# The FP4 weights' last product on GpSimd, and their maxima as the first steps of the NF4 loop's FP4 chain

## What is computed

```
x = x + LN(x) @ (weight * blockmask).T
x = x + LN(x) @ (int4 * scale).T + bias
x = x + L1_attn(LN(x))       # weights are NF4 codes * scales, plus LoRA, d_ff 1792
x = x + L1_ffn(LN(x))        # weights and activations rounded to FP4, d_ff 1376
```

```
s  = max(max|w| / 2688, 1e-12)                # one number for the whole matrix
sb = clip(max|w/s| over 16 columns / 6, ...)  # one number per block of 16
q  = nearest FP4 level of w/s/sb
dq = q * sb * s                               # the last product; the last 128 columns stay w
```

## Time and profile before

| | us |
|---|---|
| runs: lowest, median, highest of 3 | 808.89, 811.8, 812.21 |
| the profiled execution's own time | 808.92 |
| its span, first to last instruction | 807.6 |
| TensorE busy | 723.5 (90%) |
| VectorE busy | 576.0 (71%) |
| ScalarE busy | 444.6 (55%) |
| GpSimd busy | 188.6 (23%) |
| mean granted TensorE clock | 0.960 of full speed |

### The profile page before, as it was taken

The page is one execution under the profiler, slowest core; times in us unless marked ns, Lnnn a source line. Parts: engine busy times, 40 slices in busy tenths (PEclk is TensorE's granted clock), DMA queues, the critical chain, the costliest instruction groups (busy, mean ns, idle before and its releaser), DMA issues.

```text
span 807.6 us, 11305 instructions
## 1 busy us (share of the span) xinstructions
PE 723.5 (90%) x4136; PEld 538.1 (67%) x4136; DVE 576.0 (71%) x1087; ACT 444.6 (55%) x579; POOL 188.6 (23%) x174
## 2 busy tenths in 40 slices
PE   1899766988999998989998999988899999989998
PEld 1666522656777765666665777766677788967886
DVE  5979967563597788879799887666654434578883
ACT  3777877565777677876875632254433211335452
POOL 1013000004263543626356343211401000000000
PEclk9999956999999999999998999998999999989999
DMA  9637678766466676767665310302211010200001
GB/s 342 186 124 210 209 262 266 262 205 231 128 201 196 196 244 210 230 198 240 230 196 162 109 40 32 83 1 66 81 37 48 25 39 14 75 2 14 26 27 40
DMA packets 55543, 110.82 MB, mean 137 GB/s; under 512 B 9904, under 2 KB 20560, under 8 KB 55232
## 3 DMA queue, kind: packets, MB, share of 16 engines
q1 hardware_dynamic: 42912, 80.27, 31.0%
q10 hardware_dynamic: 8192, 15.73, 6.1%
q0 software_dynamic: 4384, 14.09, 5.9%
HBM read 92.17 MB, written 17.89 MB: 136 GB/s over the span
## 4 chain that ended last, share of the span: by engine, by line
PE 53%; DVE 24%; issue 9%; ACT 8%; DMA 4%; ACTq 1%; POOL 0%; SPq 0%; DVEq 0%; POOLq 0%
PE bank L1198 14%; PE bank L1199 13%; PE bank L1200 13%; PE bank L1306 3%; ACT hot L1615 2%; DVE hot L1876 2%; DMA wide_buf<-in_down_flat 2%; DVE x L1999 2%; DVE bank L1902 2%; DVE q_a L1949 1%; PE bank L1319 1%; PE bank L1504 1%; ACT c L1574 1%; DVE q_r L1943 1%; DVE stats L1798 1%
## 5 line engine op out<-in xcount | busy, mean ns | idle before, releaser
L1615 ACT ACTIVATE hot<-rep,levels 128x2048 f16<-128x2048 f16 x94 | 189.5, 2056 | 15.2 <-ACT c L1574 11.7
L1198 PE MATMUL bank<-zt_h,w_h 128*128 128x512 f32 (+1 forms) x232 | 93.2, 402 | 2.5 <-DVE zt_l L1987 2.0
L1200 PE MATMUL bank<-zt_h,w_l 128*128 128x512 f32 (+1 forms) x232 | 91.0, 392 | 0.0
L1199 PE MATMUL bank<-zt_l,w_h 128*128 128x512 f32 (+1 forms) x232 | 90.8, 392 | 0.0
L1306 PE MATMUL bank<-hot,diag 128*32 128x512 f16 x1160 | 78.7, 402 | 2.2 <-ACT hot L1615 2.2
L1198 PE MATMUL bank<-w_h,xq_h 128*128 128x512 f32 (+1 forms) x192 | 73.8, 385 | 2.3 <-ACT xq_l L1707 1.9
L1199 PE MATMUL bank<-w_l,xq_h 128*128 128x512 f32 (+1 forms) x192 | 71.9, 374 | 0.0
L1200 PE MATMUL bank<-w_h,xq_l 128*128 128x512 f32 (+1 forms) x192 | 71.7, 374 | 0.0
L2143 POOL TENSOR_TENSOR q_a<-q_a,q_m 128x384 f32<-128x384 f32 (+3 forms) x34 | 35.7, 1051 | 106.7 <-DVE q_m L1762 106.7
L1306 PEld LDWEIGHTS bank<-hot,diag 128*32 128x32 f16 x1160 | 26.4, 99 | 45.8 <-issue 24.9
L2199 POOL TENSOR_TENSOR at_l<-ztok,at_h 128x512 fp32r<-128x512 f32 x28 | 37.4, 1336 | 70.4 <-ACT at_h L1647 70.3
(11 more groups left out here) (221 smaller groups left out, 1692.0 us busy)
## 6 DMA issues: line engine op xcount, KB each, us to landing
rep<-codes SPq DMA_DIRECT2D x56, 512.0 KB, 4.7
codes<-c SPq DMA_DIRECT2D x28, 256.0 KB
raw<-in_codes_gu_t ACTq DMA_DIRECT2D x14, 512.0 KB, 5.4
sc<-in_scales_gu_t SPq DMA_DIRECT2D x56, 128.0 KB, 4.3
raw<-in_codes_attn_t ACTq DMA_DIRECT2D x7, 512.0 KB, 4.0
raw<-in_codes_down_t ACTq DMA_DIRECT2D x7, 512.0 KB, 5.3
sc<-in_scales_down_t SPq DMA_DIRECT2D x28, 128.0 KB, 3.1
wide_buf<-in_gate_flat SPq DMA_DIRECT2D x5, 512.0 KB, 4.4
```

What stands on the lines that cost most here:

```text
L1198: PE.matmul(psum, lh, rh, start=first, stop=False, **kw)
L1199: PE.matmul(psum, lh, rl, start=False, stop=False, **kw)
L1200: return PE.matmul(psum, ll, rh, start=False, stop=last, **kw)
L1615: S.activation(hots[plan.slot[hot_ring(t), (t, m)]][:], codes_in_place(t), ACT.Relu, bias=bias, scale=slope).then_inc(sem("ramp_act"), 1)
```

## The change

1. maxima() is no longer woven into stages() and attention(). It is chained ahead of fp4_weights(), as one side of the NF4 loop: its 20 yields and the 78 others are 98 for the loop's 100 main steps, and FP4_RATE goes from 0.8 to 1.0.
2. wround on GpSimd gets a third instruction, the last product. VectorE's wfinish is gone. For w_down, VectorE multiplies the block factors by mscale ahead of it (12 small instructions). The two temporary buffers (q_tmp) are freed by GpSimd's product, and SP's store waits for GpSimd.

```diff
-MAX_RATE = 1.0
-FP4_RATE = 0.8
+FP4_RATE = 1.0
...
-                p.take("q_tmp", 2, ("w", name, c, o), ("dve", "wfinish", name, c, o))
+                p.take("q_tmp", 2, ("w", name, c, o), ("pool", "wfinish", name, c, o))
...
-    fp4, greatest = fp4_weights(), maxima()
+    fp4 = itertools.chain(maxima(), fp4_weights())
...
-    side_max = Side(greatest, MAX_RATE)
-    weave(stages(), Side(itertools.chain(int4_weights(), greatest), INT4_RATE), Side(ready_nf4, EARLY_RATE))
-    until(n_attn - 1, side_max)
+    weave(stages(), Side(int4_weights(), INT4_RATE), Side(ready_nf4, EARLY_RATE))
+    until(n_attn - 1)
...
-    weave(attention(), Side(ready_nf4, ATT_RATE), side_max)
-    drain(greatest)
+    weave(attention(), Side(ready_nf4, ATT_RATE))
...
                 reciprocals(rb, cb)
+                if name == "down":
+                    V.tensor_scalar(cb, cb, mscale[:, o:o + 1], None, ALU.mult)
...
-            elif kind == "wfinish":
...
-                if name == "down":
-                    ins = V.scalar_tensor_tensor(blocks_of(wide, nq), blocks_of(ua, nq), mscale[:, o:o + 1], part,
-                                                 ALU.mult, ALU.mult)
-                else:
-                    ins = V.tensor_tensor(blocks_of(wide, nq), blocks_of(ua, nq), part, ALU.mult)
-                ins.then_inc(sem("wfinish_dve"), 1)
...
-                round_off(ua, um, nq, done("dve", "wround", *key), own).then_inc(sem("wround_pool"), 1)
+                own.up(round_off(ua, um, nq, done("dve", "wround", *key), own))
+                own.wait_ge()
+                for m in vacant("q_out", ("w", *key)):
+                    pool.wait_ge(*m)
+                G.tensor_tensor(blocks_of(q_out[plan.slot["q_out", ("w", *key)]][0:orow, :], nq), blocks_of(ua, nq),
+                                spread_of(cc[:, 0:nq // FP4_BLOCK], orow, nq), ALU.mult).then_inc(
+                                    sem("wfinish_pool"), 1)
...
-                sp.wait_ge(*done("dve", "wfinish", *key))
+                sp.wait_ge(*done("dve", "wread", *key))
+                sp.wait_ge(*done("pool", "wfinish", *key))
```

More of the change, by code:

```diff
@@ L1248, in row_buf, with blocks_of, spread_of @@
         return late_bufs[plan.slot["late", ("row", c, i)]]
+    def blocks_of(t, nq):
+        return t[:, 0:nq].rearrange("p (b c) -> p b c", c=FP4_BLOCK)
+    def spread_of(t, rows, nq):
+        return t.unsqueeze(2).broadcast_to([rows, nq // FP4_BLOCK, FP4_BLOCK])
     def wround_size(name, c, o):
@@ L1749, in reciprocals @@
             steady.wait_ge()
[L1751 to L1755, removed]
         def magic(ua, um, nq):
@@ L2193, in pool_program @@
                 orow, w, nq = wround_size(*key)
-                ua, um, _, _ = (v[0:orow, :] for v in q_tmp[plan.slot["q_tmp", ("w", *key)]])
-                round_off(ua, um, nq, done("dve", "wround", *key), own).then_inc(sem("wround_pool"), 1)
+                ua, um, cc, _ = (v[0:orow, :] for v in q_tmp[plan.slot["q_tmp", ("w", *key)]])
+                own.up(round_off(ua, um, nq, done("dve", "wround", *key), own))
[5 more added lines that the diff above has]
+                                    sem("wfinish_pool"), 1)
             elif kind == "gu_mul":
```

## The result

The changed kernel takes **817.75 us** in the median (six runs, 815.5 to 821.84) against 810.85 for the kernel before (six runs, 808.75 to 813.14) on the same chip: ratio 1.009, 95% interval [1.0064, 1.0115]. It is slower, where I had forecast no change at 811.7; the time lies in the range of 801 to 821. The profiled execution took 817.39 us with a span of 816.1, against 808.92 and 807.6.

A forecast was written before the change was run, and what follows sets the result against it. No engine was full from 60 to 139 us; TensorE was full in the loop's first 20 steps, then 225.7 of 241.7 us. Terms -1.2 - 4.5 + 9 - 1.4 + 2.5 - 4.5 = -0.1 gave 811.7 us, range 801 to 821.

The forecast's parts named there:

- The stages and attention: Before the loop, VectorE loses 18 reductions of the maxima: -1.2 us in the stages, -4.5 in attention as TensorE's gaps go.
- The loads in the head: Loop's first 20 steps: late landings of the maxima's parts cost TensorE +9 us; a gap going with the moved roundings, -1.4.
- The gather: First gather, now at step 21 behind the maximum over partitions, is wanted at step 22: TensorE waits, +2.5 us.
- The pause of GpSimd behind the gathers: GpSimd's at_l and rounding wait behind eight indirect DMAs (10 us) but are used several steps later: 0.
- The dense part: Loop's next 80 steps: product moves to GpSimd, VectorE's load hardly falls but its peaks do, so TensorE waits less: -4.5 us.
- My own sign for this: Sign of a wrong forecast: the loop's 80 steps after the first 20 take longer than 241.7 us.
- L1902's gaps: Sign of a right forecast: TensorE's waits for L1902 after the loop's first 20 steps are near 6.5 us.
- The rival with the comparisons: GpSimd blocks VectorE's comparisons, which lose 13 us instead of 2; 80 later steps cost +0.5, not -4.5: 816.7 us, chance 0.10.
- The head at the pace of the loads: Slower rival: landing, issue and reduction exceed 6.9 us, costing 13.5 in the loop's first 20 steps: 822.2 us, chance 0.22.
- the first rival: Faster rival: loads hidden, peaks were what counted; first 20 loop steps cost +1.5, the next 80 give 8: 799.7 us, chance 0.28.

The follow-up runs named there:

- four halves: The changed kernel with four halves of buffer instead of two for the maxima's parts, loads going out three parts ahead: 808.01 us, ratio 0.995.

## Why the prediction was wrong

**The stages and attention** (forecast -1.2 and -4.5): the stages' boundary moved by under 1 us and attention gave the rest of -6.1. Of the gaps of the earlier trace rows behind late parts 0.7 us is left. Right.

**The loads in the head** (+9 - 1.4): the difference is right, +7.7, by errors that cancel, which is luck. The idle time rose by 6.4 us (1.4 to 7.8), where I had 7.6; even this term had a miscount in it, for between 153 and 178 us the trace has six reductions and not seven, which makes 0.87 us a part and 10.5 for the head instead of 9. The same matmuls at a lower clock cost 4.8 us more, which no term of the sum had. And 32 transposes of seven or eight tiles left the head, worth some 3.5 us (67.88 - 64.39), which I neither credited here nor charged to the dense part.

**The gather** (+2.5): TensorE waited 1.4 us for it. Inside the bounds. The pause of GpSimd behind the gathers, which I had at 0, cost about 1 us of the dense part by the traces, too little for the times to tell.

**The dense part** (-4.5) is the step that failed: "So its load there hardly falls, since the higher rate gives back what the move takes. What falls is the peak". For VectorE's load I had 199.7 us, and 2 of contention, against 203.3; the measured load rose by 8.4 us, for seven tiles cost 29 us on VectorE with the stalls of all the others, where 2.96 each made 20.7. And equal load was not no cost: the waits for L1899 grew by 5.5 us where I had taken away 4.5. Measured one at a time, the product gives -3.5 us in the dense part, near my -4.5 though only 2.0 of it are waits for L1902. The seven tiles brought there, with the higher rate, give +12.3 (259.0 with four halves against 246.7): 6.7 of busy TensorE, of which 3 to 5 are their 29 transposes, and 5.6 of idle, of which 1.3 are the wait for the first gather. That is 1.8 us a tile, 1.4 without that wait and the pause, where in the head seven tiles cost 0.6 each (68.7 against 64.4). I had priced the seven tiles and the higher rate at nothing for TensorE. My own sign for this stood in the prediction: a dense part longer than before. L1902's gaps there were to be 6.5 us and were 16.5.

In one sum, going from kernel to kernel by their traces: the product -4.1 in the loop (319.5 to 315.4), the tiles moved out of the head, with the maxima in their place and the higher rate, +8.0 (315.4 to 323.4), the late loads +11.9 (323.4 to 335.3), the start -6.1 and the end -1.2: +8.5 us.

**The rivals.** The rival with the comparisons named nearly the right time, 816.7, and the right stage, but the wrong cause: with the product alone moved the dense part became 3.5 us shorter, and at the new rate 9.1 us. That its time fits is luck. The comparisons lost 3.4 us more than before, where it had them lose 13; more went to the small scalings of each tile (L1751 and L1943), 129 and 99 ns more in the mean for 34 tiles. The Trainium skill, "SBUF — State Buffer", Who interferes with whom, has it that when a VectorE instruction in a two-port mode and a GpSimd one meet, the later is blocked until the other is done. The trace agrees in that 11 of the 13 long L1751 ended 0.03 to 0.04 us after a GpSimd instruction; in which mode they ran no run here shows. With the product alone moved, 11 us of the 28.5 that it freed came back in other instructions or were its mscale products. The head at the pace of the loads (822.2) did not come, since VectorE waited at seven of the 18 parts only.

The kernel with the loads hidden, four halves, came to a ratio of 0.995, not the 0.985 of the first rival: its head was as hoped for, its dense part not.

## What to carry over

When side work is moved from one stretch of a loop to another, price the work pushed out of its old place as well: a rounding tile cost 0.6 us of TensorE's time in the steps where VectorE had room and 1.4 to 1.8 where it was at 84%. A double-buffered load that waits for its predecessor but one in an in-order queue needs its landing, and the queue's other waits, to fit into the distance; here two more halves, otherwise idle, were worth 11 us with the maxima in the loop (ratio 1.009 to 0.995) and 5.9 with them in attention. And of two edits that arrive together, time each alone: one was worth -0.9%, the other +1.6%.

## What the runs showed of the hardware

- **A gap can cost twice.** The granted clock read 0.66 in the 5 us behind a gap of 2.87 us of TensorE, and a head with 7.8 us of idle time needed 4.8 us more for the same matmuls than one with none (69.15 and 64.39 us). Behind the 2.30 us gap at 171 us in the kernel before it stayed at 1.00.
- **GpSimd paused for 8.95 us** between gathers that follow a partition all-reduce and its next plain addition; with a plain copy in the all-reduce's place the addition starts 0.97 us after the last gather's start. In the kernel before the addition came 8.07 us after the last gather, but there the trace has it waiting for ScalarE's at_h, so whether it paused can't be seen.
- **VectorE's small instructions stall behind GpSimd's running ones.** One of them, a scaling of 14 to 32 elements a partition (L1751), took 174 ns at the least and 1167 at the most; in 11 of the 13 long cases it ended 0.03 to 0.04 us after a GpSimd instruction that had begun before it.
- **A product with a broadcast operand was no dearer on GpSimd than an addition.** The groups of its three instructions in the changed kernel, for 384 elements:

```profile
L2131 POOL TENSOR_TENSOR q_a<-q_a,q_m 128x384 f32<-128x384 f32 x20 | 22.0, 1102 | 1.6
L2128 POOL TENSOR_TENSOR q_a<-q_a,q_m 128x384 f32<-128x384 f32 x20 | 20.4, 1019 | 31.8 <-DVE q_m L1759 31.7
L2184 POOL TENSOR_TENSOR q_d<-q_a,q_c 128x384 f32<-128x384 f32 x20 | 18.6, 932 | 1.6
```

  My bounds were 1.1 to 1.9 us; it took 0.93.
